# Row maxima and the splits of keys, values and queries move from the attention stage into the expert stage

## The reference, cut to what matters

```
xn  = layernorm(x)                           # (2, 4096, 512), 8192 tokens
ch  = layernorm((xn @ W_to_kv.T) @ W_compress.T) * gamma + beta      # 64 wide
q, k, v = rope(ch @ Wq.T), rope(ch @ Wk.T), ch @ Wv.T                # 64 wide
a   = softmax(causal(q @ k.T / 8)) @ v       # per sequence of 4096
attn = z @ W_to_kv + z @ W_out_res.T + b_out,  z = a @ W_comp2lat.T
ffn  = shared(xn) + sum over the two chosen of 16 experts of w * (silu(xn @ gate) * (xn @ up)) @ down
out = x + attn + ffn                         # all in float32
```

## Time and profile before

| | us |
|---|---|
| median of 3 runs (lowest, highest) | 2112.65 (2106.06, 2117.63) |
| the profiled execution, whole | 2114.9 |
| its span, first to last instruction | 2113.2 |
| PE busy in it | 1859.5 |
| `routed`, first silu to last silu | 786.6 to 1526.1 |
| `attend`, first instruction to the end of the span | 1540.65 to 2113.2 |

### The profile page before, as it was taken

How to read it: one execution, slowest core, us unless ns; L and a number is a source line. 1 busy time by engine, 2 the same in 40 slices (tenths; PEclk the granted TensorE clock), 3 DMA queues, 4 the chain that set the end, 5 groups by cost and what they waited for, 6 DMA issues and landing times. The chain is left out here.

```text
span 2113.2 us, 29578 instructions
## 1 busy us (share of the span) xinstructions
PE 1859.5 (88%) x8572; PEld 1450.5 (69%) x8572; DVE 1141.1 (54%) x2257; ACT 778.7 (37%) x1510; POOL 798.4 (38%) x856
## 2 busy tenths in 40 slices
PE   2899999999999969999999899999927899778997
PEld 1677777777777757777777777777715667556675
DVE  5776777767777523322222222222246788567874
ACT  2222222222222213333333333333314566745665
POOL 1544444344443413333334333333312334413343
PEclk7899999999999989999999999999958999989998
DMA  7656565655666344444444544453266654776532
GB/s 265 213 189 197 194 204 208 196 193 186 215 195 191 123 167 155 157 162 152 159 157 162 210 159 156 161 194 117 69 183 132 165 112 122 154 180 163 118 100 60
DMA packets 146998, 348.48 MB, mean 165 GB/s; under 512 B 19404, under 2 KB 41036, under 8 KB 146880
## 3 DMA queue, kind: packets, MB, share of 16 engines
q1 hardware_dynamic: 102912, 242.03, 34.4%
q0 software_dynamic: 43968, 104.91, 18.9%
HBM read 204.14 MB, written 146.67 MB: 166 GB/s over the span
## 5 line engine op out<-in xcount | busy, mean ns | idle before, releaser
L1061 POOL DMA_INDIRECT expert_rows<-res,ids_all x143 | 145.3, 1016 | 431.7 <-ACT res L1013 420.9
L1332 ACT ACTIVATE ex<-sc 128x512 f32<-128x512 f32 (+3 forms) x288 | 165.3, 574 | 161.8 <-PE sc L1238 160.5
L872 POOL DMA_INDIRECT token_list<-tok,slot x128 | 125.7, 982 | 246.3 <-DVE slot L636 210.3
L1217 PE MATMUL mb<-khl,qh 128*128 128x512 f32 (+3 forms) x288 | 116.7, 452 | 96.1 <-DVE qlm L1354 47.1
L69 PE MATMUL egu<-w,rT_0h 128*128 x576 | 189.1, 410 | 2.0 <-SPq L927 2.0
L1361 DVE TENSOR_REDUCE mx<-mb 128x1 f32<-128x512 f32 (+3 forms) x288 | 175.0, 641 | 24.3 <-PE mb L1217 20.9
L69 PE MATMUL egu<-w,rT_1h 128*128 x568 | 184.4, 406 | 0.0
L1037 DVE TENSOR_TENSOR eh<-egu,esg 128x256 f32<-128x256 f32 x143 | 60.7, 424 | 226.3 <-ACT esg L1003 226.3
L1056 POOL DMA_INDIRECT rows<-xn_scratch,rows_all x143 | 138.5, 968 | 74.1 <-issue 42.6
L1217 PEld LDWEIGHTS mb<-khl,qh 128*128 128x128 f32 x288 | 59.0, 210 | 138.5 <-DVE qlm L1354 53.4
L1003 ACT ACTIVATE esg<-egu 128x256 f32<-128x256 f32 x143 | 54.9, 384 | 232.4 <-PE egu L69 232.4
(11 more groups left out here) (284 smaller groups left out, 4826.7 us busy)
## 6 DMA issues: line engine op xcount, KB each, us to landing
w<-expert_parts SPq DMA_DIRECT2D x64, 768.0 KB, 7.8
base<-expert_rows POOLq DMA_DIRECT2D x32, 1024.0 KB, 12.4
expert_parts<-ew_h SPq DMA_DIRECT2D x32, 768.0 KB, 3.3
expert_parts<-ew_l SPq DMA_DIRECT2D x32, 768.0 KB, 5.7
x<-x SPq DMA_DIRECT2D x16, 1024.0 KB, 5.3
xn_scratch<-xn SPq DMA_DIRECT2D x16, 1024.0 KB, 5.9
base_scratch<-xb SPq DMA_DIRECT2D x16, 1024.0 KB, 5.3
base<-base_scratch SPq DMA_DIRECT2D x16, 1024.0 KB, 8.9
```

The source lines that it names most:

```text
L872: pool.indirect_dma_start(list_d[:, :], bass.IndirectOffsetOnAxis(ap=slot[q][:, j, c:c + 1], axis=0), tok[q][:, j, c, :], None).then_inc(s ...
L1061: pool.indirect_dma_start(parts_d[:, :], bass.IndirectOffsetOnAxis(ap=ids_all[:, t:t + 1], axis=0), res[t % 2][:, :], None, bounds_check=2 ...
L1217: mm = pe.matmul(mb[g % 2][:, 0:w], qh[n % 2][:, j * P:(j + 1) * P], khl[:, key:key + w], start=True, stop=(c < m))
L1332: i = act.activation(dst[:, off:GROUP], sc[u % NSC][:, off:GROUP], ACT.Exp, scale=SCALE)
```

## The change

`routed` now also computes all 288 row maxima (`max_scores`, `reduce_max`), between the tiles of slots 3 to 137, two or three units per slot, one of them behind `turn` and the others ahead of it. It splits the queries, keys and values (`split_high`, `split_low`), four steps for each group in four slots, and loads them by transfers that ACT issues (`load_block`). The two banks for `emb` come from `ehb` and `edb`, which now have one buffer each. The maxima are turned once (`turn_lowest`) and stored to `row_maxima` in DRAM. The constants of `attend` (`mop`) are computed at the start of `routed`, POOL clears `kh1` there, and the gathers have eight buffers. `attend` then only loads the queries again, with the row of maxima, and works in steps over all groups: two key blocks of 128 to a step (1024 columns for ACT, DVE and POOL), one on the diagonal, with two buffers for `sc` (two banks each) and `ex`, three for `pr`, two for `ob`, and `LAG` 2. A group's end no longer stops the next group's scores.

```diff
-AHEAD = 4
+AHEAD = 8
...
+FIRST_SLOT, LAST_SLOT = 3, TILES - 6
...
+    done = -(-FIRST_MAX[NG] * (t + 1 - FIRST_SLOT) // (LAST_SLOT + 1 - FIRST_SLOT))
+    return min(FIRST_MAX[NG], max(0, done))
...
+        tb, gu, mb = [[ps(f"e{n}{i}") for i in range(2)] for n in ("tb", "gu", "mb")]
+        hb, db = ps("ehb"), ps("edb")
...
+        group_of = [n for n in range(NG) for _ in range(GT * KEY_GROUPS[n])]
+        slot_of = [next(t for t in range(TILES) if maxima_until(t) > FIRST_MAX[n]) for n in range(NG)]
+        split_slot, later = {}, TILES
+        for n, which in ((n, which) for n in range(NG - 1, 0, -1) for which in range(3, -1, -1)):
+            later = split_slot[n, which] = min(later, slot_of[n] - 4 + which)
+        splits = [sorted(step for step in split_slot if split_slot[step] == t) for t in range(TILES)]
+        loads = [[n for n in range(2, NG) if slot_of[n - 2] == t] for t in range(TILES)]
...
+            done, until = maxima_until(t - 1), maxima_until(t)
+            return range(done, (done + until + 1) // 2), range((done + until + 1) // 2, until)
...
+            for dst, src in ((wz, w_kv), (wo, w_outT), (wc[:, :], w_c2l), (wv[:, :], w_vT), (gam[:, :], gamma), (bet[:, :], beta),
+                             (fold[:, 0, :], fold_in), (tri[:, :], tri_in[1])):
+                sp.dma_start(dst, src).then_inc(const_in, 16)
             load(0, 0, None)
...
-                after(pe, d_ev, t if t > 1 else 0)
-                mm = parts(pe, db[t % 2][:, :], [([a[:, k, :] for a in hT[t % 2]],
-                                                  [weights(b, a, k, 4 * FE) for a in range(2)]) for k in range(FK)])
+                after(pe, d_ev, t + 1 if t else 0)
...
-                after(pe, hT_lo, t - 1)
+                after(pe, hT_lo, t)
...
+                some, others = maxima(t)
                 gate_up(t)
                 if t > 0:
                     down(t - 1)
                 pe.reg_mov(last_buffer, this_buffer)
                 if t + 1 < TILES:
                     find_buffer(t + 1)
+                if t == FIRST_SLOT:
+                    pe.wait_ge(bias_ready, 1)
+                    pe.wait_ge(mo_ev, 4)
+                for g in some:
+                    max_scores(g)
                 if t + 2 < TILES:
                     turn(t + 2)
+                for g in others:
+                    max_scores(g)
+                if t == LAST_SLOT + 2:
+                    turn_lowest()
                 turn_hidden(t)
...
+            def load_block(n):
+                q, at = n % 2, slice(n * GROUP, (n + 1) * GROUP)
+                after(act, highs, 4 * (n - 1))
+                after(act, k_low, n - 1)
+                after(act, v_low, n - 1)
+                for half in (slice(0, C), slice(C, P)):
+                    act.dma_start(ka[q][half, :], k_d[:, at]).then_inc(qkv_in[q], 16)
+                    act.dma_start(qa[q][half, :], q_d[:, at]).then_inc(qkv_in[q], 16)
+                act.dma_start(va[q][:, :, :].rearrange("p j c -> p (j c)"), v_d[n]).then_inc(qkv_in[q], 16)
...
                 silu(t)
+                for n in loads[t]:
+                    load_block(n)
                 if t + 2 < TILES:
                     turned(t + 2)
                 if t > 0:
                     downed(t - 1)
+                for n, which in splits[t]:
+                    split_high(n, which)
                 hidden_turned(t)
...
             for t in range(TILES):
+                some, others = maxima(t)
                 hidden(t)
+                for g in some:
+                    reduce_max(g)
                 if t + 2 < TILES:
                     turned(t + 2)
+                for g in others:
+                    reduce_max(g)
+                for n, which in splits[t]:
+                    split_low(n, which)
                 hidden_turned(t)
...
+            for t in range(AHEAD - 4):
+                gather(t)
+            pool.memset(value(kh1[C:P, :]), 0.0).then_inc(blank, 1)
+            pool.wait_ge(blank, 1)
+            pool.memset(value(kh1[C:C + 1, :]), 1.0).then_inc(blank, 1)
+            for t in range(AHEAD - 4, AHEAD):
...
+        NE, NP, NQ, NB = 2, 3, 3, 4
+        LAG = 2
...
+        steps = [(n, kb, 2) for n in range(0)]
+        for n in range(NG):
+            own = GT * (n % QB)
+            steps += [(n, kb, 2) for kb in range(0, own, 2)] + [(n, own + d, 1) for d in range(GT)]
+        by_pool = [count == 2 and n % QB >= 2 and kb // 2 % 4 == 1 for n, kb, count in steps]
...
+        finish = {first[n + 1] - 1 + LAG: n for n in range(NG)}
+            gap = max(1, (first[n + 2] - first[n + 1]) // GT) if n + 2 <= NG else 1
+            for j in range(GT):
+                project_at[first[n + 1] + LAG + 1 + j * gap] = (n, j)
...
+            for n in range(NQ):
+                load_queries(n)
             for n in range(NB):
                 load_base(n)
             for n in range(NG):
-                if n + 2 < NG:
-                    load_block(n + 2)
+                if 2 <= n < NG - NB + 2:
+                    load_base(n - 2 + NB)
+                if n + NQ < NG:
+                    load_queries(n + NQ)
...
+            for i in range(TAIL):
+                if i < len(steps):
+                    scores(i)
+                if LAG <= i < len(steps) + LAG:
+                    outputs(i - LAG)
+                if i in project_at:
+                    project(*project_at[i])
```

More of the change, by code:

```diff
@@ L1157, in attend @@
-        start = [1 if u == GT else 3 if u == 2 * GT else 5 for u in units]
-        def steps(n):
-            ahead = units[n + 1] if n + 1 < NG else 0
-            over = units[n] - 2 - start[n]
-            for kb in range(units[n]):
-                behind = [j for j in range(GT) if n and kb == min(1 + j * (n % QB + 1), units[n] - 1)]
-                yield kb, range(*(min(ahead, max(0, -(-ahead * k // over))) for k in (kb - start[n], kb - start[n] + 1))), behind
+            if by_pool[i]:
+                eng.wait_ge(pool_low, pool_before[i] + 1)
+            else:
+                eng.wait_ge(dve_low, i - pool_before[i] + 1)
@@ L1168, in attend, with make_low @@
+        def make_low(eng, i):
+            eng.wait_ge(e_done, i + 1)
+            after(eng, sel_done, diagonal(i))
+            after(eng, pv_done, i - NP + 1)
+            eng.tensor_tensor(prp[i % NP][1][:, span(i)], ex[i % NE][:, span(i)], value(prp[i % NP][0][:, span(i)]),
+                              ALU.subtract).then_inc(pool_low if by_pool[i] else dve_low, 1)
         block = ctx.enter_context(nc.Block())
@@ new lines, in outputs @@
+            def outputs(i):
+                n, kb, count = steps[i]
+                low_there(pe, i)
+                if i == first[n]:
+                    after(pe, o_ev, n - 1)
+                to = span(i).start
+                for c in range(count):
+                    b, at = n // QB * QB + (kb + c) // GT, slice(c * GROUP + to, (c + 1) * GROUP)
+                    for a in range(2):
+                        mm = pe.matmul(ob[n % 2][:, to:GROUP], vhl[:, b, (kb + c) % GT, :], prp[i % NP][a][:, at],
+                                       start=(kb + c == 0 and a == 0), stop=(i + 1 == first[n + 1] and a == 1))
+                mm.then_inc(pv_done, 1)
@@ new lines, in exps, with output_high @@
+            def exps(i):
+                act.wait_ge(s_done, i + 1)
+                low_there(act, i - NE)
+                after(act, pv_done, i - NP + 1)
+                for dst in (ex[i % NE], prp[i % NP][0]):
+                    e = act.activation(dst[:, span(i)], sc[i % 2][:, span(i)], ACT.Exp, scale=SCALE)
+                e.then_inc(e_done, 1)
+            def output_high(n):
+                act.wait_ge(pv_done, first[n + 1])
+                after(act, p_done, GT * (n - 1))
+                act.copy(oT[n % 2][0][:, :], ob[n % 2][:, :]).then_inc(o_hi, 1)
```

516 lines of the change are left out of this document (243 added, 273 removed).

## The result

The change made the kernel faster by 1.7%, where 5.6% were forecast: 2076.67 us median of 4 runs against 2113.53, ratio 0.983 with a 95% interval of 0.980 to 0.986. The profiled execution has a span of 2073.5. First its stretches (the columns are those of the earlier trace rows), then the tile `esg`, which stands beside the earlier trace rows, and the waits of PE in `routed`, beside the earlier trace rows.

What follows compares the result with a forecast made beforehand. PE was taken to pace `routed`, PE and DVE to share the limit in `attend`; +46 us in `routed` and -165 in `attend` turned 2113.2 into 1994, said as 1995 with 1.7 outside the span; range 1940 to 2065.

Steps and rivals of the forecast that it cites:

- ACT and DVE between PE's products: In routed: later hT_l and rT_l, beyond the slack ahead of PE's products, with late scatters cost 15 us, bounds 0 to 60.
- Maxima, +67: In routed: PE's 288 units of row maxima add 67 us, bounds 64 to 90.
- Gathers, -42: In routed: with eight buffers the waits for gathers go, saving 42 us, between 32 and 48.
- The start, +6: Start of routed: the constants' chain ends a little behind the first weights, +6 us, or +15 if POOL's clears are slow.
- POOL's low parts, 25: In attend: exps wait 0.85 us for POOL's low parts in each of 30 steps, 25 us in sum.
- PE's work, 291: In attend: PE's matmuls over sixteen groups, 3.65m + 5.9 each, make 299 us, 8 of them done during the start.
- The start, 40: Start of attend: 40 us until the first combine, for issuing and landing base and its two additions.
- the second sequence: In attend: the second sequence's short groups ask for base faster than it lands, and clears stand behind POOL's waits: 12 us.
- transfers bind `attend`: Rival: transfers set the pace of attend's short groups; each sequence loses 20 us more, 2035 to 2040 us; chance 0.14.
- the diagonals: In attend: on diagonal blocks the low part comes late behind POOL's clearing, two waits a group, 20 us in all.
- Slower: Rival: in routed PE waits for DVE every slot; the change is lost if the chain is 1.6 us longer; chance 0.06.
- no-effect: Rival: attend keeps its pace as ACT waits for low parts every step, 0.7 us longer each, within 0.5%; chance 0.04.

Runs made afterwards that it cites:

- reads_ahead: The changed kernel with PE's two table reads of a slot moved from behind the down product to ahead of it: 2030.96 us, 0.962 of the kernel before.
- three: The changed kernel with all low parts in attend on DVE, table reads ahead of the down product, POOL's kh1 clears behind all eight first gathers: 2000.36 us, 0.947.
- no_adds: The changed kernel without the additions of the experts' rows to the base in attend (output lacks the experts' part): 2042.47 us, 0.966 of the kernel before.
- three_no_adds: The kernel `three` without the additions of the experts' rows in attend (output lacks the experts' part): 1958.86 us, 0.927 of the kernel before.

## Why the prediction was wrong, step by step

Of the 79 us, 23 belong to the first step below, 11 to the maxima, 8 to the start, 3 to the change of stages and 35 to `attend`; the gathers gave 2 more than taken.

*ACT and DVE between PE's products* (the failed step). The prediction counted a slack of 0.87 from `hT_l` to the down product, reduced it to 0.6, and charged only what would go beyond: 15 us. The shift was about right (0.67 measured). But the slack was already in use: behind `down` PE's sequencer reads the table for the next tile, and the reads are hidden only if the product is released about 1.0 us before its matmuls start. Each 0.1 less of slack costs 0.1 of every slot. That was legible in the earlier trace rows as 0.09 between the sixth `edb` matmul and `etb`, and was passed over. Against the kernel before with eight buffers, the distance from the first `edb` to the next product grew from 1.47 to 1.69 (slots 5 to 135), 32 us over 142 slots; with 6 more in the gate and up products, 38 stand where the term had 15. Moving the reads gave back 47.4 us of the silu rows: this growth, some 12 that the kernel with eight buffers also loses there, and some 9 of the units' time, less 7 that then appear in the gate and up products. The view of waits names no engine for it: it says "issue".

*Maxima, +67*: mis-sized by 11. From the distances of starts in the same slots, the units (with 0.07 less at `etb`) take 0.58 a slot in the changed kernel, 78 us over 135 slots; with the reads moved 0.51, 69 us. That `reads_ahead` takes 765.5 us, the "some 765" forecast for the changed kernel, is luck: it has also lost a gap that the kernel before has. *Gathers, -42*: right, 44.4. Most of what they gain was taken by the reads.

*The start, +6*: mis-sized, +14. The clears take 6.92 us on POOL, as taken; the gathers were not late. But a clear held the product with gamma for 6.2 us, of which moving it gives back 5.5; the rest is the constants' landing, 18 us after the end of `prepare`. The Trainium skill (Trainium Architecture — The Big Picture, What this means for kernel authors) says that DVE and POOL share a port pair under an exclusive lock. The row of 6.46 agrees; that the two-input subtraction of 0.69 beside the clear in `three` is not held shows that it does not touch all of DVE's operations.

*POOL's low parts, 25*: nearly right, 29; with the additions out they cost 38 (`attend` takes 411.7 us in `no_adds`, 374.0 in `three_no_adds`). *PE's work, 291*: right for the long groups, with steps of 1.85 where 1.83 stood: the last one takes 31.6 from output copy to output copy in `three_no_adds`, and 3.65 x 7 + 5.9 with 1.25 for its diagonal makes 32.7. *The start, 40, and the second sequence, 12*: not too small. The first `combine` comes 36.1 us into the stage. Some 34 of the 52 stood for the additions (12 and 10 to land, 12 later), and leaving them out gives back 31 (442.3 against 411.7), or 42 without POOL's low parts (416.5, 374.0).

*What else failed in `attend`*: the forecast gave a group its PE work and its share of the diagonals, with 5 us for the clock in all, and the short groups take longer. Without the terms for additions and low parts the forecast is 348, and `three_no_adds` takes 374.0, 26 more (14, if the 12 of the second sequence are left in). Half of that stands in three short groups: from output copy to output copy, groups 1, 8 and 9 take 14.4, 11.4 and 16.3 us there, where the forecast's terms make 10.8, 7.2 and 10.8. PE's clock is at 0.77 and 0.70 in the first two, and in the last two PE waits 3.1 us for `combine` ahead of projections, whose result `pj` has one buffer. No run isolates either, so the cause of the 26 stays open. The other 9 of the 35 us are additions and low parts together (68 us against 59).

The rival "transfers bind `attend`" describes what the short groups do: the share of DMA is 0.99 in the first 64 us and 0.90 from 1890 to 1950. But it put 40 on top of the 34 that stood in the sum, and the 31 to 42 measured are all that the additions cost. The argument against it, that `base` is loaded earlier, concerned the wrong transfer: the landings of `base` fell from 8.9 to 6.9, those of the additions rose from 12.3 to 13.2, and the short groups issue them in a row:

```profile
1642.52 1.44 POOL L1516 DMA_DIRECT2D base<-expert_rows  x1 [21.98 <-DMA base<-base_scratch]
...
1656.63 1.26 POOL L1516 DMA_DIRECT2D base<-expert_rows  x1 [6.05 <-DMA base<-expert_rows]
1662.42 2.58 POOL L1516 DMA_DIRECT2D base<-expert_rows  x2 [4.52 <-DMA base<-expert_rows]
...
1678.40 2.62 POOL L1516 DMA_DIRECT2D base<-expert_rows  x2 [7.21 <-DMA base<-expert_rows]
```

The queues of the changed kernel from 1636 to 2060 (packets, MB, share of 16 engines' time):

```profile
q0 software_dynamic: 16896, 33.56, 44.5%
q1 hardware_dynamic: 18624, 36.18, 24.9%
```

The 32 additions are the first: 0.445 of 424 us over 32 is 5.9 us of all engines each, where the plain transfers (0.249 of it for 36.2 MB) take 3.1 for as many bytes. That the additions alone go through POOL's queue is not the reason: in `routed` (800 to 1614) the gathers and scatters of the same queue take 0.247 of 814 us for 69.5 MB, 3.0 for as many bytes. A group with two additions, a load and a store then needs 18.0 us of transfers; groups 1, 2 and 8 took 20.6, 21.7 and 18.5.

*Slower and no-effect rivals*: neither occurred. Still the first was nearer to the truth than its condition said: it let the chain be 1.6 us late before the change would be lost, and with both units behind `turn` the kernel was 81 us slower than the changed one and 46 slower than the kernel before, without `edb` waiting in most slots (15 times of 143).

## What to carry to other kernels

A slack in front of a product is free only if nothing behind it on the same engine lives on being reached early. So read the distance behind the product too. Take a 0.1 us gap marked "issue", or not marked at all, as a sign that the slack may be spent. Put register reads from memory ahead of the semaphore wait, not behind it. Sum the transfers' time over the shortest phases, with the accumulating ones at their own price, instead of over the stage. When a run leaves work out, take its terms out of the forecast too before the two are compared. Before a helper engine is given a share of the work, see whether the main one is short of time at all.

## What the runs showed of the hardware

- The same 64x64 DVE product with a scalar took 0.24 us alone and 6.46 beside a POOL memset; two-input DVE subtractions beside such a memset kept their 0.69, but beside POOL's own two-input subtraction one took 1.67 in place of 1.23.
- PE's two table reads start some 0.65 us behind the release of the product ahead of them and take 1.1 to 1.2, and the next matmul follows 0.5 to 0.7 later. Behind six matmuls (1.36 us) they are hidden only with about 1.0 us of slack. Placed ahead of the product's wait, they leave a gap of 0.02.
- The rows of a memset of 64x8192 are 6.92 us on POOL and 6.88 on DVE. But a second memset that waits for the first starts 0.06 behind its row on POOL and 1.76 behind it on DVE (8.65 from start to start).
- An accumulating transfer of 1 MB takes the DMA engines 1.9 times as long as a plain one: 5.9 us against 3.1 (5.8 and 3.5 in the kernel before).
